# A four-layer graph network on one core: first-layer inputs loaded in the edge-list block, score products as five groups on two sets of PSUM banks

## The chip, the cores and the metric

The kernel runs on one core of one Trainium2 chip. The metric is the device time of one execution in microseconds (us), and its median before the change is 2970.07 us over three runs (2968.24 to 2970.22). Engines are named as the profile names them: PE is TensorE's matmul side and PEld its weight load, DVE is VectorE, ACT is ScalarE, POOL is GpSimd, SP is SyncE. A name with a q behind it (SPq, PEq) is the sequencer of that engine, which waits, branches and issues DMAs.

## The reference

There are 3125 nodes with 64 features and 103125 edges sorted by their receiving node. Four layers follow each other, each ending in `x = layernorm(x + layer(x))`. The change touches only the start of the first:

```python
proj = einsum('nf,hfg->nhg', x, w_proj)                 # 4 heads
delta = proj[sender] - proj[receiver]
radial_logits = einsum('ehf,hf->eh', delta, radial_score) - scale * edge_len
tangential_logits = einsum('ehf,hf->eh', delta, tangential_score)
...  # segment softmax of both over the receiver, summed over delta
```

The part of a logit that depends on the receiver cancels in the softmax. What is left of a sender is the product of its 64 features with one vector per head and score, `u = sum_g w_proj[h, f, g] * score[h, g]`. So the kernel needs `u` (64 x 8) and `x @ u` for all nodes (3125 x 8), once.

## The kernel before

Nodes are laid out as 25 windows of 128 (`NW` is 25, `P` 128). The program is a sequence of blocks; in a block each engine has its own instruction stream, ordered by semaphores, and all engines meet in a barrier at its end. Where a phase frees its semaphores (L65, L66), a second barrier follows.

The order of work is this.

- The edge-list block (L541 to L701) loads source, destination and weight of all edges (SP, L548 to L552), turns them on PE (L692), and then runs some 80 small DVE instructions in a chain up to L684, which pack the loops' bounds. SP waits for two tables (L557), stores them (L558, L559) and waits for everything it has issued (L560, L561).
- The score block (L722 to L743) starts after the two barriers. SP issues six loads: `w_proj`, the two scores, the distance scale and the node features `x` in two pieces (L726 to L732). DVE waits for all six (L738), then multiplies and reduces twice to get `u` (L740, L741) and scales the edge lengths (L742, L743).
- `node_linear` (L124 to L178) computes `x @ u` in five turns of `U` = 5 windows, as a hardware loop on each engine. In a turn POOL copies five windows to `staged` (L140), PE transposes them into PSUM `turned_ps` (L150), ACT copies that to SBUF `turned` (L165), PE multiplies it by `u` into `out_ps` (L155), and DVE copies the result to `logits` (L174). There is one `turned_ps`, one `turned` and one `out_ps`.
- The following block (L747 to L810) takes the largest and smallest logit over all nodes, exponentiates, scales the features by it, and stores the table that the edges gather from (L757).
- The first edge loop (`edges0`, from L860) gathers a table row per edge with indirect DMAs that POOL issues (L880), 888 of them. Then come the end of the first layer, the second layer (`rounds`), and the second edge loop with its own 888 indirect DMAs (L2066). The last stage (from L2394) holds a group of five transposes, a copy and five products like that of `node_linear`, written out and not as a loop (L2445, L2417, L2453), with a bias row and 64 output columns.

All SP DMAs of these blocks go through SP's one queue, in program order.

Of the kernel before, what the change touches and what calls it, by code (L numbers as in the profile page):

```python
# [14 lines left out]
P = 128  # L15
# [193 lines left out]
def build(nc, a, out):  # L209
    with Phase(nc, "all") as whole:  # L210
# [285 lines left out]
        with Phase(nc, "first") as first:  # L496
# [7 lines left out]
            with Borrowed(nc, "setup", flat) as ph:  # L504
                x_in = ph.sb("x_in", [P, NW, F])
                lens = ph.sb("lens", [P, TT])
                with Borrowed(nc, "strips", flat, ph.at) as pt:
                    FULL = TILES // P * P
# [32 lines left out]
                    with nc.Block() as block:  # L541

                        @block.sync
                        def _(sp):
# [13 lines left out]
                            sp.dma_start(src_kept, src_i[:, :]).then_inc(s_kept, 16)  # L558
                            sp.dma_start(dst_kept, dst_f[:, :]).then_inc(s_kept, 16)  # L559
                            sp.wait_ge(s_ld, 144)  # L560
                            sp.wait_ge(s_kept, 48)  # L561

                        @block.gpsimd
# [138 lines left out]

                w_proj = ph.sb("w_proj", [F, H0, F])
                score = ph.sb("score", [F, 2, H0 * F])
                prod = ph.sb("prod", [F, H0, F])
                u = ph.sb("u", [F, A0])
                neg_c = ph.sb("neg_c", [P, 1])
                logits = ph.sb("logits", [P, NW, A0])
# [5 lines left out]
                factor_t = ph.sb("factor_t", [P, NW, H0])  # L714
                s_ld, s_ch, s_less, s_exp, s_rows = (ph.sem(n) for n in ("s_ld", "s_ch", "s_less", "s_exp", "s_rows"))
                s_top, s_all, s_st, s_neg = ph.sem("s_top"), ph.sem("s_all"), ph.sem("s_st"), ph.sem("s_neg")
# [5 lines left out]
                with nc.Block() as block:  # L722

                    @block.sync
                    def _(sp):
                        sp.dma_start(w_proj[:, :, :], a["L0_gnn_w_proj"].rearrange("h f g -> f h g")).then_inc(s_ld, 16)  # L726
                        for n, name in enumerate(("L0_gnn_radial_score", "L0_gnn_tangential_score")):
                            sp.dma_start(score[:, n], a[name].rearrange("h f -> (h f)").partition_broadcast(F)).then_inc(s_ld, 16)
                        sp.dma_start(neg_c[:, :], a["L0_gnn_radial_distance_scale"].partition_broadcast(P)).then_inc(s_ld, 16)
                        with nc.allow_non_contiguous_dma("rows"):  # L730
                            sp.dma_start(x_in[:, 0:FULLW, :], by_node(a["x"][0:FULLW * P])).then_inc(s_ld, 16)
                            sp.dma_start(x_in[0:RESTW, FULLW, :], a["x"][FULLW * P:N]).then_inc(s_ld, 16)  # L732
                        sp.wait_ge(s_ld, 96)

                    @block.vector
                    def _(dve):
                        step = Chain(dve, s_ch)
                        dve.wait_ge(s_ld, 96)  # L738
                        for n in range(2):
                            step(dve.tensor_tensor(prod[:, :, :], w_proj[:, :, :], score[:, n].rearrange("p (h f) -> p h f", f=F), ALU.mult))  # L740
                            step(dve.tensor_reduce(u[:, n * H0:(n + 1) * H0], prod[:, :, :], AX, ALU.add))  # L741
                        step(dve.tensor_scalar(neg_c[:, :], neg_c[:, :], -1.0, None, ALU.mult))  # L742
                        step(dve.tensor_scalar(lens[:, :], lens[:, :], neg_c[:, 0:1], None, ALU.mult))  # L743

                node_linear(nc, lambda nc, tag: Borrowed(nc, tag, flat, ph.at), "l0", x_in, u[:, :], F, A0, None, logits)

# [1810 lines left out]
```

## Time and profile before

| | us |
|---|---|
| median of three runs | 2970.07 |
| lowest, highest | 2968.24, 2970.22 |
| the profiled execution, its own time | 2972.75 |
| its span, first to last instruction | 2970.9 |
| first edge loop, first to last indirect DMA's start | 144.4 to 1296.3 |
| PE, DVE, POOL busy | 75%, 70%, 60% of the span |

The times of instructions below are counted from the start of the span. A share of busy time is an average over stages that have different limits, so the stretch that the change touches is read by itself, in order of time. An idle time in square brackets is how long the engine had nothing to do before an instruction, with what released it.

### The profile page before, as it was taken

The numbers are of one execution on the slowest core, as the hardware profiler recorded it, in microseconds if no ns is written. First come the engines' busy times: TensorE is split into PE (matmuls) and PEld (weight loads), VectorE is DVE, ScalarE is ACT, GpSimd is POOL, SyncE is SP. The second block draws the span as 40 slices with busy tenths as digits, with TensorE's granted clock in tenths as the row PEclk, the third lists the DMA queues.
The fourth block names the chain that finished last, engine by engine and source line by source line (L and its number), as shares of the span: only waits on it lengthen the run. The fifth ranks groups of instructions, "written<-read, shape, count | busy, mean of one in ns | idle before, by whom it ended". The sixth has DMA issues, their size and how long they took to land. (4 is left out here: it accounts for less than half of the span.)

```text
span 2970.9 us, 64636 instructions
## 1 busy us (share of the span) xinstructions
PE 2225.6 (75%) x13922; PEld 1710.1 (58%) x13923; DVE 2083.0 (70%) x7862; ACT 631.7 (21%) x1180; POOL 1783.2 (60%) x1857
## 2 busy tenths in 40 slices
PE   0288888889888898986799557667676676676748
PEld 0255555555555555555799446656566666565637
DVE  6477777777777777747566557777777777777755
ACT  0323322333222333231000111111111111111100
POOL 0077777777777777730001167777777777777722
PEclk9999999999999999985899555555555555555558
DMA  1144554545545455542000133333333333333330
GB/s 42 55 128 133 141 142 128 142 130 145 141 129 143 126 142 141 134 88 57 20 1 2 35 77 83 81 82 82 81 81 82 81 83 81 81 82 80 82 41 12
DMA packets 425511, 268.62 MB, mean 90 GB/s; under 512 B 334070, under 2 KB 375909, under 8 KB 425445
## 3 DMA queue, kind: packets, MB, share of 16 engines
q0 software_dynamic: 71040, 176.52, 23.6%
q1 hardware_dynamic: 284418, 49.42, 8.8%
q10 hardware_dynamic: 69986, 41.88, 4.6%
q8 instruction: 32, 0.52, 0.1%
q14 instruction: 35, 0.28, 0.0%
HBM read 231.16 MB, written 15.97 MB: 83 GB/s over the span
## 5 line engine op out<-in xcount | busy, mean ns | idle before, releaser
L880 POOL DMA_INDIRECT edges_rows<-table,edges_idx x888 | 862.8, 972 | 290.2 <-issue 221.9
L2066 POOL DMA_INDIRECT all_arena<-table_kv,edges_idx x888 | 855.8, 964 | 276.3 <-issue 255.7
L2258 PE MATMUL edges_acc<-edges_values,edges_into 128*128 128x136 f32 x1776 | 511.4, 461 | 259.7 <-DVE edges_values L2146 237.6
L2258 PEld LDWEIGHTS edges_acc<-edges_values,edges_into 128*128 128x128 f32 x1776 | 416.6, 328 | 307.0 <-DVE edges_values L2146 286.4
L1053 PE MATMUL edges_radial_ps<-edges_rows,edges_into_w 128*128 x1776 | 461.3, 396 | 94.1 <-SPq L897 75.3
L962 DVE TENSOR_SCALAR edges_cell<-edges_ramp,edges_strip_key,first_key 128x400 bf16<-128x400 f16 x1184 | 451.2, 381 | 0.0
L1053 PEld LDWEIGHTS edges_radial_ps<-edges_rows,edges_into_w 128*128 128x128 f32 x1776 | 319.8, 190 | 219.0 <-issue 178.0
L2111 DVE TENSOR_SCALAR edges_ahead<-edges_nodes,edges_starts,edges_dst_f 128x128 bf16<-128x128 f32 x894 | 261.7, 360 | 174.3 <-issue 174.3
L961 DVE TENSOR_SCALAR edges_low<-edges_places,first_src_low 128x128 bf16<-128x128 bf16 x1184 | 332.1, 281 | 0.0
L2192 ACT COPY edges_into_t<-edges_t_ps 128x384 bf16<-128x384 bf16 x298 | 142.9, 480 | 874.0 <-PE edges_t_ps L2226 865.1
L967 DVE TENSOR_SCALAR edges_into_w<-edges_nodes,first_dst_f,first_weight 128x128 f32<-128x128 f32 x888 | 276.1, 368 | 0.0
L1048 PE MATMUL edges_cells_ps<-edges_cell,edges_low 128*128 128x400 bf16 x1184 | 251.2, 335 | 32.9 <-DVE edges_cell L962 25.7
L2120 DVE TENSOR_SCALAR edges_into<-edges_nodes,edges_starts,edges_dst_f 128x128 f32<-128x128 f32 x891 | 257.5, 350 | 20.5 <-PE edges_acc L2258 19.2
L2226 PE MATMUL edges_t_ps<-all_ident,edges_ahead 128*128 128x128 bf16 x894 | 155.1, 312 | 112.2 <-DVE edges_ahead L2111 110.0
L1023 PE MATMUL edges_tan_ps<-all_arena 128*128 128x393 bf16 x1300 | 232.0, 335 | 0.1
L1114 ACT ACT_TABLE_LOAD x50 | 64.2, 1283 | 727.3 <-PE edges_radial_ps L1053 727.3
L2235 PE MATMUL edges_q_ps<-attention_q,edges_into_t 128*128 (+1 forms) x2673 | 206.6, 244 | 0.0
L2226 PEld LDWEIGHTS edges_t_ps<-all_ident,edges_ahead 128*128 128x128 bf16 x894 | 108.8, 144 | 153.2 <-DVE edges_ahead L2111 99.0
L1048 PEld LDWEIGHTS edges_cells_ps<-edges_cell,edges_low 128*128 128x128 bf16 x1184 | 101.3, 98 | 162.9 <-DVE edges_cell L962 105.1
L2235 PEld LDWEIGHTS edges_q_ps<-attention_q,edges_into_t 128*128 128x128 bf16 x2673 | 188.5, 134 | 1.1
L1023 PEld LDWEIGHTS edges_tan_ps<-all_arena 128*128 128x128 fp8e4 x1300 | 129.5, 102 | 87.8 <-issue 4.4
L1159 POOL TENSOR_TENSOR rounds_st<-rounds_st,all_minus_half 128x5 f32<-128x5 f32 x20 | 25.9, 1295 | 226.0 <-DVE rounds_st L1150 226.0
(343 smaller groups left out, 2561.4 us busy)
## 6 DMA issues: line engine op xcount, KB each, us to landing
edges_values<-in_edge_attr SPq DMA_DIRECT2D x888, 32.0 KB
all_arena<-all_arena ACTq DMA_DIRECT2D x50, 400.0 KB
edges_rows<-table,edges_idx POOLq DMA_INDIRECT x888
all_arena<-table_kv,edges_idx POOLq DMA_INDIRECT x888
edges_attr<-in_edge_attr ACTq DMA_DIRECT2D x51, 256.0 KB
edges_bias<-bias_kept SPq DMA_DIRECT2D x296, 12.0 KB
bias_kept<-edges_bias_out ACTq DMA_DIRECT2D x52, 64.0 KB
table<-all_arena SPq DMA_DIRECT2D x1, 3250.0 KB, 11.4
```

Source lines behind the costliest of these rows:

```text
L880: pool.indirect_dma_start(rows[:, n, :], None, table0, bass.IndirectOffsetOnAxis(ap=idx[:, n:n + 1], axis=0)).then_inc(s_rows[g], 16)
L961: dve.tensor_scalar(low[:, h, q, :], places[:, :], src_low[:, bass.ds(tile[q], 1)], None, ALU.is_equal)
L962: last = dve.tensor_scalar(cell[:, h, q, :], ramp[:, :], strip_key[:, q:q + 1], key[:, bass.ds(tile[q], 1)], ALU.add, ALU.is_equal)
L967: last = dve.tensor_scalar(into_w[:, h, j, :], nodes[:, :], dst_f[:, bass.ds(t, 1)], weight[:, bass.ds(t, 1)], ALU.is_equal, ALU.mult)
L1023: last = nc.tensor.matmul(tan_ps[:, 0:3 * TAN], last_count[:, c, :], parts0[:, side * NW + c, :, :].rearrange("p k f -> p (k f)"), start=( ...
L1048: nc.tensor.matmul(cells_ps[:, q, 0:KEY], low[:, h, q, :], cell[:, h, q, :], start=False, stop=True, skip_group_check=True)
L1053: last = nc.tensor.matmul(radial_ps[:, 0:ROW0], into_w[:, h, j, :], rows[:, bass.ds(slot + h * G + j, 1), :].squeeze(1), start=False, stop ...
L2066: pool.indirect_dma_start(rows[:, n, :], None, table_kv, bass.IndirectOffsetOnAxis(ap=idx[:, n:n + 1], axis=0)).then_inc(s_rows[g], 16)
L2111: last = dve.tensor_scalar(ahead[:, h, j, :], nodes[:, :], starts[:, bass.ds(w, 1)], dst_f[:, bass.ds(base + h * G + j, 1)], ALU.add, ALU. ...
L2226: last = nc.tensor.transpose(t_ps[:, h, j * P:(j + 1) * P], ahead[:, h, j, :], ident16[:, :])
L2235: last = nc.tensor.matmul(q_ps[:, h, j * F:(j + 1) * F], into_t[:, h, j, :], q3[:, bass.ds(w, 1), n, :].squeeze(1), start=(n == 0), stop=( ...
L2258: last = nc.tensor.matmul(acc[:, 0:2 * F + H2], into[:, h, j, :], values[:, h, j, :], start=False, stop=True, skip_group_check=True)
```

## The change

The six loads move from the score block into the edge-list block, behind the two table stores on SP's queue, with a semaphore of their own (`s_first`, 96) that SP waits for before the block ends. Their tiles `w_proj`, `score` and `neg_c` are laid out ahead of the tiles of that block so that they do not overlap them. The score block has no SP part and no wait left. `node_linear` isn't called here any more; its place is taken by a block with five groups written out. PE transposes straight from `x_in`, so POOL's copy to `staged` is gone. There are two `turned_ps`, two halves of `turned` and two `out_ps`, and PE's order is: transposes of group 0, transposes of group 1, products of 0, transposes of 2, products of 1, and so on to the products of 3 and 4.

```diff
@@ -504,6 +504,10 @@
             with Borrowed(nc, "setup", flat) as ph:
                 x_in = ph.sb("x_in", [P, NW, F])
                 lens = ph.sb("lens", [P, TT])
+                w_proj = ph.sb("w_proj", [F, H0, F])
+                score = ph.sb("score", [F, 2, H0 * F])
+                neg_c = ph.sb("neg_c", [P, 1])
+                s_first = ph.sem("s_first_in")
                 with Borrowed(nc, "strips", flat, ph.at) as pt:
                     FULL = TILES // P * P
                     REST = TILES - FULL - 1
@@ -557,8 +561,16 @@
                             sp.wait_ge(s_tab, 2)
                             sp.dma_start(src_kept, src_i[:, :]).then_inc(s_kept, 16)
                             sp.dma_start(dst_kept, dst_f[:, :]).then_inc(s_kept, 16)
+                            sp.dma_start(w_proj[:, :, :], a["L0_gnn_w_proj"].rearrange("h f g -> f h g")).then_inc(s_first, 16)
+                            for n, name in enumerate(("L0_gnn_radial_score", "L0_gnn_tangential_score")):
+                                sp.dma_start(score[:, n], a[name].rearrange("h f -> (h f)").partition_broadcast(F)).then_inc(s_first, 16)
+                            sp.dma_start(neg_c[:, :], a["L0_gnn_radial_distance_scale"].partition_broadcast(P)).then_inc(s_first, 16)
+                            with nc.allow_non_contiguous_dma("rows"):
+                                sp.dma_start(x_in[:, 0:FULLW, :], by_node(a["x"][0:FULLW * P])).then_inc(s_first, 16)
+                                sp.dma_start(x_in[0:RESTW, FULLW, :], a["x"][FULLW * P:N]).then_inc(s_first, 16)
                             sp.wait_ge(s_ld, 144)
                             sp.wait_ge(s_kept, 48)
+                            sp.wait_ge(s_first, 96)
 
                         @block.gpsimd
                         def _(pool):
@@ -700,11 +712,8 @@
                             act.copy(dst_f[:, :], turn_ps[:, 1, 0:TT]).then_inc(s_copied, 1)
                             act.copy(lens[:, :], turn_ps[:, 2, 0:TT]).then_inc(s_copied, 1)
 
-                w_proj = ph.sb("w_proj", [F, H0, F])
-                score = ph.sb("score", [F, 2, H0 * F])
                 prod = ph.sb("prod", [F, H0, F])
                 u = ph.sb("u", [F, A0])
-                neg_c = ph.sb("neg_c", [P, 1])
                 logits = ph.sb("logits", [P, NW, A0])
                 top = ph.sb("top", [P, 2, A0 + 1])
                 top_all = ph.sb("top_all", [P, 2, A0 + 1])
@@ -712,7 +721,7 @@
                 rows = ph.sb("rows", [P, NW, ROW0])
                 factor_r = ph.sb("factor_r", [P, NW, H0])
                 factor_t = ph.sb("factor_t", [P, NW, H0])
-                s_ld, s_ch, s_less, s_exp, s_rows = (ph.sem(n) for n in ("s_ld", "s_ch", "s_less", "s_exp", "s_rows"))
+                s_ch, s_less, s_exp, s_rows = (ph.sem(n) for n in ("s_ch", "s_less", "s_exp", "s_rows"))
                 s_top, s_all, s_st, s_neg = ph.sem("s_top"), ph.sem("s_all"), ph.sem("s_st"), ph.sem("s_neg")
                 s_part, s_cast = ph.sem("s_scaled"), ph.sem("s_parts")
 
@@ -720,29 +729,55 @@
                     return parts0[:, k * NW:(k + 1) * NW, n, :]
 
                 with nc.Block() as block:
-
-                    @block.sync
-                    def _(sp):
-                        sp.dma_start(w_proj[:, :, :], a["L0_gnn_w_proj"].rearrange("h f g -> f h g")).then_inc(s_ld, 16)
-                        for n, name in enumerate(("L0_gnn_radial_score", "L0_gnn_tangential_score")):
-                            sp.dma_start(score[:, n], a[name].rearrange("h f -> (h f)").partition_broadcast(F)).then_inc(s_ld, 16)
-                        sp.dma_start(neg_c[:, :], a["L0_gnn_radial_distance_scale"].partition_broadcast(P)).then_inc(s_ld, 16)
-                        with nc.allow_non_contiguous_dma("rows"):
-                            sp.dma_start(x_in[:, 0:FULLW, :], by_node(a["x"][0:FULLW * P])).then_inc(s_ld, 16)
-                            sp.dma_start(x_in[0:RESTW, FULLW, :], a["x"][FULLW * P:N]).then_inc(s_ld, 16)
-                        sp.wait_ge(s_ld, 96)
 
                     @block.vector
                     def _(dve):
                         step = Chain(dve, s_ch)
-                        dve.wait_ge(s_ld, 96)
                         for n in range(2):
                             step(dve.tensor_tensor(prod[:, :, :], w_proj[:, :, :], score[:, n].rearrange("p (h f) -> p h f", f=F), ALU.mult))
                             step(dve.tensor_reduce(u[:, n * H0:(n + 1) * H0], prod[:, :, :], AX, ALU.add))
                         step(dve.tensor_scalar(neg_c[:, :], neg_c[:, :], -1.0, None, ALU.mult))
                         step(dve.tensor_scalar(lens[:, :], lens[:, :], neg_c[:, 0:1], None, ALU.mult))
 
-                node_linear(nc, lambda nc, tag: Borrowed(nc, tag, flat, ph.at), "l0", x_in, u[:, :], F, A0, None, logits)
+                with Borrowed(nc, "logit", flat, ph.at) as pt:
+                    turned = pt.sb("turned", [F, 2, U * P])
+                    turned_ps = [pt.ps(f"turned_ps{i}", [F, 8, P]) for i in range(2)]
+                    out_ps = [pt.ps(f"out_ps{i}", [P, U, A0]) for i in range(2)]
+                    s_tps, s_turned, s_lin, s_read = (pt.sem(n) for n in ("s_turned_ps", "s_turned", "s_linear", "s_read"))
+                    GR = NW // U
+                    with nc.Block() as block:
+
+                        @block.tensor
+                        def _(pe):
+                            for g in range(GR + 1):
+                                if g < GR:
+                                    if g >= 2:
+                                        pe.wait_ge(s_turned, g - 1)
+                                    for n in range(U):
+                                        last = nc.tensor.transpose(turned_ps[g % 2][:, n, :], x_in[:, g * U + n, :], ident[:, :])
+                                    last.then_inc(s_tps, 1)
+                                if g:
+                                    pe.wait_ge(s_turned, g)
+                                    if g >= 3:
+                                        pe.wait_ge(s_read, g - 2)
+                                    for n in range(U):
+                                        last = nc.tensor.matmul(out_ps[(g - 1) % 2][:, n, :], turned[:, (g - 1) % 2, n * P:(n + 1) * P], u[:, :],
+                                                                start=True, stop=True)
+                                    last.then_inc(s_lin, 1)
+
+                        @block.scalar
+                        def _(act):
+                            for g in range(GR):
+                                act.wait_ge(s_tps, g + 1)
+                                if g >= 2:
+                                    act.wait_ge(s_lin, g - 1)
+                                act.copy(turned[:, g % 2, :].rearrange("p (n i) -> p n i", i=P), turned_ps[g % 2][:, 0:U, :]).then_inc(s_turned, 1)
+
+                        @block.vector
+                        def _(dve):
+                            for g in range(GR):
+                                dve.wait_ge(s_lin, g + 1)
+                                dve.tensor_copy(logits[:, g * U:(g + 1) * U, :], out_ps[g % 2][:, :, :]).then_inc(s_read, 1)
 
                 with nc.Block() as block:
```

## Rows read from the trace of the kernel before

**Rows 1.** The page: the span, and the granted clock of 40 slices.

```profile
span 2970.9 us, 64636 instructions
...
PEclk9999999999999999985899555555555555555558
```

**Rows 2.** The page's costliest groups: POOL's indirect DMAs of both edge loops.

```profile
L880 POOL DMA_INDIRECT edges_rows<-table,edges_idx x888 | 862.8, 972 | 290.2 <-issue 221.9
L2066 POOL DMA_INDIRECT all_arena<-table_kv,edges_idx x888 | 855.8, 964 | 276.3 <-issue 255.7
```

**Rows 3.** Timeline, 35 to 73 us: start, duration, engine, line, operation, idle time before.

```profile
35.21 0.58 DVE L615 TENSOR_SCALAR all_arena<-all_arena 128x812 int32<-128x812 int32 x1
35.56 0.43 SPq L559 DMA_DIRECT2D dst_kept<-first_dst_f  x1
...
60.01 0.17 DVE L684 COPY all_visits<-all_arena 1x25 int32<-1x25 int32 x1
61.17 0.79 SPq L726 DMA_DIRECT2D all_arena<-in_L_gnn_w_proj  x1
...
64.38 2.24 SPq L732 DMA_DIRECT2D all_arena<-in_x  x1
69.63 0.42 DVE L740 TENSOR_TENSOR all_arena<-all_arena 64x256 f32<-64x256 f32 x1 [9.45 <-DMA all_arena<-in_x]
...
71.61 0.64 DVE L743 TENSOR_SCALAR all_arena<-all_arena 128x812 f32<-128x812 f32 x1
```

**Rows 4.** Timeline, 73 to 97 us: first two turns of `node_linear`, and its end.

```profile
73.07 0.45 POOL L140 COPY all_arena<-all_arena 128x320 f32 x1 [38.44 <-PEq L144]
...
73.66 1.25 PE L150 MATMUL l_turned_ps<-all_ident,all_arena 128*64 128x128 f32 x5 [54.59 <-POOL all_arena L140]
75.02 0.69 ACT L165 COPY all_arena<-l_turned_ps 64x640 f32<-64x640 f32 x1 [53.60 <-PE l_turned_ps L150]
...
75.76 2.30 PE L155 MATMUL l_out_ps<-all_arena 64*128 64x8 f32 x10 [0.85 <-ACT all_arena L165]
...
77.99 1.27 PE L150 MATMUL l_turned_ps<-all_ident,all_arena 128*64 128x128 f32 x5
...
93.17 2.30 PE L155 MATMUL l_out_ps<-all_arena 64*128 64x8 f32 x10 [0.85 <-ACT all_arena L165]
95.64 0.20 DVE L174 TENSOR_SCALAR all_arena<-l_out_ps 128x40 f32 x1 [4.15 <-PE l_out_ps L155]
96.60 0.51 DVE L770 TENSOR_REDUCE all_arena<-all_arena 128x8 f32<-128x200 f32 x1 [0.75 <-PEq L66]
```

**Rows 5.** SP's waits, 30 to 75 us: for what, us in total, times, longest.

```profile
SPq L561 <- DMA dst_kept<-first_dst_f: 3.1, 1, 3.1
SPq L722 <- DMA all_arena<-in_x: 3.0, 1, 3.0
```

**Rows 6.** Lines L155 and L150 alone: single durations in ns, least, median, most.

```profile
L155 PE MATMUL l_out_ps<-all_arena x50: 357/358/379, 75.8 to 95.1; 64*128 64x8 f32 x50
...
L150 PE MATMUL l_turned_ps<-all_ident,all_arena x25: 394/420/421, 73.7 to 91.9; 128*64 128x128 f32 x25
```

**Rows 7.** Timeline, 2875 to 2880 us: the written-out group of the last stage.

```profile
2875.17 1.27 PE L2445 MATMUL last_banks_turned_ps<-all_ident,attention_attn 128*64 128x128 f32 x5 [17.01 <-DVE attention_attn L2472]
2877.22 2.40 PE L2453 MATMUL last_banks_out_ps<-attention_w_sq,last_turned 65*128 65x64 f32 x10 [0.78 <-ACT last_turned L2417]
```

**Rows 8.** Windows: us, busy PE, PEld, DVE, ACT, POOL, granted clock, DMA share, GB/s.

```profile
70.00:80.00 10.00, 4.75 (x20) 3.63 (x20) 2.28 (x7) 1.31 (x2) 1.35 (x3) 1.00 0.00 0
...
1600.00:1620.00 20.00, 20.00 (x236) 19.98 (x234) 11.05 (x29) 2.10 (x4) 1.35 (x2) 1.00 0.01 2
1620.00:1635.00 15.00, 11.01 (x120) 10.60 (x117) 8.26 (x20) 1.74 (x3) 2.67 (x2) 0.99 0.00 1
1635.00:1650.00 15.00, 10.09 (x40) 8.23 (x41) 10.82 (x24) 2.06 (x3) 3.41 (x3) 0.50 0.00 1
```

**Rows 9.** Line L880 alone: durations in ns, least, median and most.

```profile
L880 POOL DMA_INDIRECT edges_rows<-table,edges_idx x888: 940/947/1297, 144.4 to 1296.3; - x178
```

## The prediction

> **What bounds the kernel now.** I first asked whether time saved at the start can reach the end. Most of the span is two edge loops, each paced by POOL: 888 indirect DMAs of 972 ns on average with 290.2 us of idle time between them, so 1.30 us a piece and 1153 us in the first loop; the second has 855.8 + 276.3 = 1132 us [rows 2]. Their start is what matters, not when in the run it falls. Between the changed stretch and the first loop there are only chains closed by barriers of all engines, and none of them waits for a DMA started before that stretch. So a microsecond taken out before 96.6 us should come off the end too, unless something later answers to it.
>
> Then I read the stretch itself in order of time. The reader is to see two holes. DVE ends the edge-list chain at 60.18, SP issues its first load at 61.17 and its last until 66.62, and DVE gets its first instruction at 69.63, after 9.45 us of idle time that the load of `x` ended [rows 3]. In the product, PE is the busiest engine, but stops before each group of products for 0.85 us, while ACT copies the turned windows [rows 4]. It first starts at 73.66, after POOL's copy. The stretch ends with DVE's L770 at 96.60 [rows 4].
>
> **Part 1, the six loads.** Their wait goes, and what then comes last is the barrier. SP was past it at 61.17; DVE leaves the same barrier. The same pair of barriers at the end of `node_linear` let DVE go 0.76 us after its last instruction (95.84 to 96.60) [rows 4], which would give 60.94. I take 61.17: 69.63 - 61.17 = 8.46 us saved; bounds 8.46 and 8.69.
>
> What the loads cost in their new place: SP's queue is free from 35.99, when the second table store is issued [rows 3]. The six issues took 66.62 - 61.17 = 5.45 us and the last load ended 3.0 us behind the last issue [rows 3, 5]. So they are issued by 41.4 and landed by about 44.5. The stores share the DMA engines for a while, and SP waited 3.1 us for them [rows 5]; even with that added, the loads are in by 48, 12 us before DVE reaches 60.18. Nothing stands behind them on SP's queue but the waits at the block's end, and the stores are ahead of them. If that cover were gone, each microsecond past 60.18 would be paid in full. For DVE working beside the transfers, the nearest row is L615, 0.58 us for 812 elements while a store is issued [rows 3]; I take nothing, with 0.3 us against me as the other end (some 25 us of DVE work slowed by 1%).
>
> DVE's six instructions from L740 to L743 stay as they are: 69.63 to 72.25, 2.62 us [rows 3].
>
> **Part 2, the start of the product.** Before, DVE ended at 72.25; then came the barrier, POOL's loop start, its copy at 73.07 of 0.45 us, and PE at 73.66 [rows 3, 4]. POOL's idle time there was ended by PE's sequencer (L144, the increment that PE gives ahead of its loop), so PE was through the barrier before 73.07. Afterwards PE's first transpose waits for nothing but the barrier. A barrier pair took 0.76 us [rows 4], so this single one ends no earlier than about 72.6. I take 72.85: 0.8 us saved, bounds 0.56 and 1.0.
>
> **Part 3, the five groups.** Before, PE ran from 73.66 to 95.47, 21.81 us: a first turn of 2.10 to the products, then 2.23 from products to transposes, and 2.12 back, of which 0.85 idle [rows 4]. A single transpose shows 0.42 us and five together 1.25 to 1.27, so their pitch is 0.21; a single product instruction 0.36 and ten together 2.30, pitch 0.216 [rows 4, 6]. Five transposes thus take 1.07 from start to next start, ten product instructions 2.16, and with a change of kind 2.23. For transposes followed at once by products no row exists. It lies between 1.07 (nothing extra) and 1.27 (the last one drained first); I take 1.17, the pitch plus a little more than the 0.07 that the other change of kind costs.
>
> The new order gives 1.07 (group 0) + 4 x 1.17 (groups 1 to 4, each ahead of products) + 3 x 2.23 (products 0 to 2, each ahead of transposes) + 2.16 + 2.30 (products 3 and 4) = 16.90 us. Saved: 21.81 - 16.90 = 4.9 us, bounds 4.4 and 5.3.
>
> That sum needs ACT's copies hidden. A group of products may start 0.85 us after its transposes end (0.69 us copy and two handoffs) [rows 4]. Products 0 stand behind group 1's transposes, which end a good microsecond after group 0's, so about 0.2 us is to spare. Later copies have at least a group of products to hide in. If the spare is negative it costs a few tenths once. DVE's copy is 0.20 us against 3.4 us until its PSUM buffer is written again. The end is unchanged: the last products, then DVE 0.17 us later, then the barriers [rows 4]. POOL's five copies of 0.45 us go and free nothing, because four of them ran behind PE's products.
>
> That written-out code runs no slower than the loop is shown by the last stage, where five transposes take 1.27 us, and the wait before the products is 0.78 [rows 7].
>
> **Sum.** 8.46 + 0.8 + 4.9 = 14.2 us; with all bounds on one side 13.1 and 15.0. The profiled execution took 2972.75 us, so its like would take 2958.6; it was 2.7 us above the median of 2970.07. Against the median: 2970.07 - 14.2 = **2955.9 us**. A difference of 0.2%, 5.9 us, is about what a measurement of this kernel can tell from no change.
>
> **Rivals.**
>
> *The clock of a later stage is dealt anew.* After the first loop the granted clock moves between 1.2 and 2.4 GHz, and the slices show mixed levels there [rows 1]. PE is fully busy at 1.00 up to 1620 us, 73% busy in the next 15 us, and then at 0.50 [rows 8]. If that fall came 10 us earlier or later in the program, ten microseconds of PE work at half rate, 5 us, would be lost or won: 2961 or 2951. For it: the fall lies close behind a stretch of dense work. Against it: four executions lie within 4.5 us. I give 0.08 to the loss and 0.05 to the gain. The Trainium skill (TensorE: Matmul & The Clock Gate, Part 1: The HAM clock gate) says that the window by which the gate is set is free-running and doesn't restart with the kernel, so an earlier start can't keep the old phase; the rows show the level changing but not its phase, and by that rule the small shifts would differ from one execution to the next.
>
> *Only the loads' part is won.* If each group of products still waited for its copy (a semaphore that comes late, or a PSUM write held by a reader), the product block would keep its turns: 2970.07 - 8.46 = 2961.6. Against it: the waits named in the diff are all due well before they are reached. Chance 0.04.
>
> *The gain is swallowed.* The change does what it says, but the first loop starts no earlier, or settles 14 us later. The first loop's indirect DMAs would need 14.2 / 888 = 16 ns more each; their mean is already 25 ns above their median of 947 [rows 2, 9], so such amounts exist. Result 2970, chance 0.05.
>
> *Slower.* The same mechanism, larger. The long indirect DMAs, up to 1297 ns [rows 9], come when DVE and POOL meet in a bad phase. The instruction streams ahead of the loops change in length and the tiles shift; if the share of long ones doubled, the first loop would gain 888 x 25 ns = 22 us: 2955.9 + 22 = 2978. It decides from 8 ns on both loops' 1776 DMAs (14.2 us), and it is slower by over 0.2% from 11 ns. Against it: the loops' code and data are untouched and start from the same barrier. Chance 0.04.
>
> **How the numbers follow.** The forecast has 0.74. Faster by over 0.2%: the forecast, both clock cases and the loads alone, 0.91. Within 0.2%: 0.05. Slower: 0.04. The forecast's own bounds are 2955.1 to 2957.0, to which the spread of medians adds a microsecond. The range takes in the clock cases and the loads alone: 2951 to 2962, leaving out 0.09 and what small shifts I haven't named.
>
> **What would show it.** In the trace after: SP's six loads right behind L559's store and landed before 50 us; DVE's first product within 1.1 us of the chain's last instruction; PE without idle time between groups and some 17 us from first transpose to last product; no POOL copy; DVE's first reduction near 82.4 us instead of 96.60. Then the first indirect DMA at 144.38 - 14.2 = 130.2 and both loops as long as before. Wrong would be: DVE waiting for a load at 60 us, PE waiting for ACT in every group, or a first loop whose POOL mean is not 972 ns.

## The result, and the profile after

The changed kernel takes 2961.69 us (median of 20 runs, 2954.46 to 2967.55), the kernel before 2970.08 us (median of 20 beside them, one disturbed run of 7149 us left out of the comparison). The ratio is 0.997, with a 95% interval of 0.9963 to 0.9977. The change is 8.4 us faster by the two medians, and 6.8 to 11.0 us by the interval, where 14.2 us was forecast. The profiled execution took 2963.00 us by its own time, 9.75 us less than that of before.

The page of after, to be held against [rows 1, 2]; the columns of the two groups are busy us, mean ns, idle us before:

```profile
span 2960.8 us, 64538 instructions
...
L915 POOL DMA_INDIRECT edges_rows<-table,edges_idx x888 | 867.7, 977 | 291.2 <-issue 227.9
L2101 POOL DMA_INDIRECT all_arena<-table_kv,edges_idx x888 | 855.9, 964 | 276.6 <-issue 257.3
```

The second loop's line stands where it stood. The first loop's has grown by 4.9 us of busy time and 1.0 us of idle time, on lines that the change didn't touch. That is the missing part. First the changed stretch itself, in the timeline of after (start, duration, engine, line, operation, idle time before), to be read against [rows 3, 4]:

```profile
35.38 0.79 SPq L564 DMA_DIRECT2D all_arena<-in_L_gnn_w_proj  x1
...
38.71 2.25 SPq L570 DMA_DIRECT2D all_arena<-in_x  x1
...
59.36 0.17 DVE L696 COPY all_visits<-all_arena 1x25 int32<-1x25 int32 x1
60.56 0.42 DVE L737 TENSOR_TENSOR all_arena<-all_arena 64x256 f32<-64x256 f32 x1 [1.04 <-PEq L66]
...
63.72 2.31 PE L757 MATMUL logit_turned_ps<-all_ident,all_arena 128*64 128x128 f32 x10 [45.58 <-PEq L731]
...
65.96 2.30 PE L764 MATMUL logit_out_ps<-all_arena 64*128 64x8 f32 x10
...
68.19 1.27 PE L757 MATMUL logit_turned_ps<-all_ident,all_arena 128*64 128x128 f32 x5
...
69.40 2.30 PE L764 MATMUL logit_out_ps<-all_arena 64*128 64x8 f32 x10
...
76.26 4.43 PE L764 MATMUL logit_out_ps<-all_arena 64*128 64x8 f32 x20
...
80.73 0.20 DVE L780 COPY all_arena<-logit_out_ps 128x40 f32<-128x40 f32 x1 [1.94 <-PE logit_out_ps L764]
81.66 0.51 DVE L805 TENSOR_REDUCE all_arena<-all_arena 128x8 f32<-128x200 f32 x1 [0.73 <-PEq L66]
...
129.41 1.30 POOL L915 DMA_INDIRECT edges_rows<-table,edges_idx  x1 [0.20 <-issue]
```

DVE's wait of 9.45 us for `x` is now 1.04 us for the barrier. PE's lines follow each other with no idle time and no wait for ACT. The first indirect DMA starts at 129.41 instead of 144.38, 14.97 us earlier, of which 0.65 us was there before the change could act (the list chain ends at 59.36 and not at 60.01, and was as far ahead before the first of the moved loads was issued). By stage, from the two timelines (starts in us):

| stage | before | after | saved | forecast |
|---|---|---|---|---|
| last list instruction to DVE's first product | 9.62 | 1.20 | 8.42 | 8.46 |
| first product to PE's start | 4.03 | 3.16 | 0.87 | 0.8 |
| PE's start to its end | 21.81 | 16.97 | 4.84 | 4.9 |
| PE's end to the first reduction | 1.13 | 0.97 | 0.16 | 0 |
| first reduction to first indirect DMA | 47.78 | 47.75 | 0.03 | 0 |
| first loop, first to last indirect DMA | 1151.92 | 1157.75 | -5.83 | 0 |
| from there to the second loop's first | 424.11 | 421.95 | 2.16 | 0 |
| second loop | 1125.26 | 1125.31 | -0.05 | 0 |
| from its last to the end of the span | 125.18 | 126.34 | -1.16 | 0 |

The front gave 14.3 us, as forecast. The first loop took 5.8 us back.

Inside that loop, DVE's groups of 120 to 1310 us differ in two lines. L975 (L940 before) is DVE's first engine instruction in each of the 25 windows of 128 nodes, and each time DVE's sequencer has set up the window's registers ahead of it. L993 (L958 before) copies the indices for the next chunk. After:

```profile
L975 DVE TENSOR_SCALAR edges_nodes<-edges_nodes 128x128 f32<-128x128 f32 x25 | 6.4, 257 | 98.8 <-issue 98.8
...
L993 DVE COPY edges_idx<-first_src_i x296 | 60.6, 205 | 99.4 <-issue 64.3 <-PE edges_radial_ps L1088 20.6 <-SPq L932 14.4
```

and before:

```profile
L940 DVE TENSOR_SCALAR edges_nodes<-edges_nodes 128x128 f32<-128x128 f32 x25 | 5.7, 228 | 102.2 <-issue 102.2
...
L958 DVE COPY edges_idx<-first_src_i x296 | 60.6, 205 | 92.3 <-issue 76.5 <-PE edges_radial_ps L1053 14.0 <-SPq L897 1.6
```

Ahead of that instruction DVE is idle for 102.2 us in 25 windows before and for 98.8 us after, and "issue" says that it waits for nothing the profile shows, which here is its own sequencer. Taken singly, the first window's idle time is 10.71 us before and 10.27 after, the 24 others are 3.79 to 3.82 and 3.67 to 3.70. So DVE's first instruction comes 0.12 us sooner at each change of window in the changed kernel, and yet DVE then waits longer for rows and for PE (99.4 against 92.3 us), and POOL's DMAs are longer. I used this sum of 25 idle times as the mark of a loop in all that follows: in all 14 traces it is either 98.8 to 98.9 or 102.0 to 102.4 us.

### The profile page after: what moved, and what is told of

It reads as the page before. It is cut to its first block and busy times, and to the rows that moved or that the text cites. A ratio compares the mean times of both kernels' runs of the same rounds, so it can differ in the third digit from the quotient of the medians.

```text
span 2960.8 us, 64538 instructions
## 1 busy us (share of the span) xinstructions
PE 2223.9 (75%) x13922; PEld 1710.8 (58%) x13923; DVE 2085.0 (70%) x7862; ACT 631.9 (21%) x1180; POOL 1785.7 (60%) x1852
## 5 line engine op out<-in xcount | busy, mean ns | idle before, releaser
L915 POOL DMA_INDIRECT edges_rows<-table,edges_idx x888 | 867.7, 977 | 291.2 <-issue 227.9
L2227 ACT COPY edges_into_t<-edges_t_ps 128x384 bf16<-128x384 bf16 x298 | 142.5, 478 | 875.9 <-PE edges_t_ps L2261 862.8
L1002 DVE TENSOR_SCALAR edges_into_w<-edges_nodes,first_dst_f,first_weight 128x128 f32<-128x128 f32 x888 | 271.9, 371 | 0.0
```

Source lines behind the costliest of these rows:

```text
L915: pool.indirect_dma_start(rows[:, n, :], None, table0, bass.IndirectOffsetOnAxis(ap=idx[:, n:n + 1], axis=0)).then_inc(s_rows[g], 16)
L1002: last = dve.tensor_scalar(into_w[:, h, j, :], nodes[:, :], dst_f[:, bass.ds(t, 1)], weight[:, bass.ds(t, 1)], ALU.is_equal, ALU.mult)
```

## The experiments

The question was what makes the first loop longer, since nothing in it was changed. The theories, with the letters that the recorded expectations use: **place** (S: the instruction streams ahead of the loop have another length, so the loop's code lies elsewhere), **start time** (T: the loop meets something else at 129 us than at 144 us), **chip** (C: executions on some chips have it), **one part** (the groups or the loads bring it), and later **total length** of DVE's stream (L) and **moment** of entry (M: some tenths of a us).

### The two parts alone

e1 keeps the early loads and calls `node_linear` again:

```diff
-                with Borrowed(nc, "logit", flat, ph.at) as pt:
...
+                node_linear(nc, lambda nc, tag: Borrowed(nc, tag, flat, ph.at), "l0", x_in, u[:, :], F, A0, None, logits)
```

> Only the loads are moved; the product stays the loop of five turns. The stretch up to the first reduction over the logits should lose 9.1 us (DVE waits 1.0 us and not 9.5). If removed time arrives at the end whole: 2970.1 - 9.1 = 2961 us. If the first edge loop's length depends on how the instruction streams lie (theory S), it may differ from 1151.9 us although nothing in it is changed; SP's, DVE's and PE's streams change little here, so S expects a loop close to that of the kernel before. If it depends on when the loop starts (theory T), a loop that starts 9 us earlier should be as long and as scattered as that of the changed kernel, 1157.8 us, and the total some 2966 us.

e2 is the kernel before with the written-out groups in place of that call:

```diff
-                node_linear(nc, lambda nc, tag: Borrowed(nc, tag, flat, ph.at), "l0", x_in, u[:, :], F, A0, None, logits)
+                with Borrowed(nc, "logit", flat, ph.at) as pt:
...
```

> Only the product is changed into five overlapped groups, the loads stay where they were. PE from first transpose to last product 17.0 us and not 21.8, and its start 0.8 us sooner: 5.7 us less up to the first reduction over the logits. Whole gain at the end: 2964.4 us. Theory S (streams): POOL's, ACT's, DVE's and PE's streams lie as in the changed kernel, so the first edge loop should have its length, 1157.8 us, and its scatter of 13 us over executions: 2970 us. Theory T (start time): a start 5.7 us earlier gives something between, 2964 to 2968 us.

e1: 2962.74 us, ratio 0.9974 (0.9964 to 0.9984). Its first indirect DMA starts at 135.57, 8.8 us earlier than before, and its median is 7.8 us below that of the kernel before beside it (2970.56), so most of it reaches the end; its loop takes 1153.15 us. e2: 2970.47 us, ratio 0.9998 (0.9989 to 1.0007). Its first indirect DMA starts at 138.47, 5.9 us earlier, and all of that is lost (0.1 us between the medians): its loop takes 1159.29 us. Their rows for the group at the window's start:

```profile
L937 DVE TENSOR_SCALAR edges_nodes<-edges_nodes 128x128 f32<-128x128 f32 x25 | 5.7, 230 | 102.4 <-issue 102.4
```

```profile
L978 DVE TENSOR_SCALAR edges_nodes<-edges_nodes 128x128 f32<-128x128 f32 x25 | 6.6, 263 | 98.9 <-issue 98.9
```

The first is e1's and has the value of before, the second is e2's and has that of after. The long loop comes with the written-out groups, also without the loads. But the groups are over long before the loop begins, so it's something that they leave behind.

### The same kernel again, and held back

e3 is the changed kernel once more. e4 lets it start its loop as late as before, with three fills of a tile that isn't in use yet:

```diff
                         step = Chain(dve, s_ch)
+                        step(dve.memset(rows[:, :, :], 0.0))
+                        step(dve.memset(rows[:, :, :], 0.0))
+                        step(dve.memset(rows[:, 0:HOLD, :], 0.0))
```

> The changed kernel once more, for a second trace. Median near 2961.7 us, spread of about 10 us. If the loss sits in the first edge loop in every execution, that loop is again over 1154 us, and at other places than in the first trace (there one turn of 17.77 us at 833 us, and 45 turns that were 0.06 us longer each). If the first trace was a chance hit, the loop is 1152 us and the loss sits elsewhere.

> The changed kernel with three fills of a tile that is not used yet put ahead of the score products on DVE, about 15 us of dead time, so that the first edge loop starts when it did in the kernel before (144 us). DVE's stream is three instructions longer, all others are those of the changed kernel. Theory T: the loop is that of the kernel before, 1151.9 us, scatter 4 us, total 2970 us. Theory S: the loop is that of the changed kernel, 1157.8 us, total 2961.7 + 15 = 2976.7 us, scatter 10 us.

e3: 2962.57 us, ratio 0.9977 (0.9968 to 0.9986), loop 1160.24 us, mark 98.8. The changed kernel has the long loop again. e4: 2974.37 us, ratio 1.001 (1.0001 to 1.0019). Its first indirect DMA starts at 147.03, which is 17.6 us later than in after, but it ends only 11.8 us behind e3's median: its loop takes 1152.31 us, as before. These rows are e4's, DVE at the window's start and POOL's DMAs:

```profile
L979 DVE TENSOR_SCALAR edges_nodes<-edges_nodes 128x128 f32<-128x128 f32 x25 | 5.7, 228 | 102.1 <-issue 102.1
```

```profile
L919 POOL DMA_INDIRECT edges_rows<-table,edges_idx x888 | 861.7, 970 | 291.7 <-issue 223.1 <-DVE edges_idx L997 68.6
```

So the written-out groups don't bring the long loop by themselves. e4 can't tell the later start from the three instructions that it adds to DVE's stream. e1 already speaks against the start time (short at 135.6, while e2 is long at 138.5); the next runs add instructions at no cost in time.

### Cheap instructions ahead of the loop

e5, e6 and e7 add one, two and four fills of a single column, each about 0.06 us, ahead of the score products:

```diff
                         step = Chain(dve, s_ch)
+                        for i in range(PAD):
+                            dve.memset(top[:, 0, i:i + 1], 0.0)
```

> The changed kernel with one fill of a single column put on DVE ahead of the score products (60 ns). The last runs split the kernels by DVE's restart at a half-window of the first edge loop (from the end of the overflow maximum to the next copy of indices): 4.95 and 5.71 us in turn with a loop of 1152 to 1153 us in before, loads only and held, 4.97 to 5.06 and 5.63 to 5.69 us with 1158 to 1160 us in the changed kernel and groups only. DVE's static stream has 174 instructions ahead of that loop in the long ones, 175, 175 and 177 in the short ones. Theory S, now narrowed to DVE's stream: one instruction more gives the 4.95 / 5.71 pattern, a loop of 1152 to 1153 us and 2961.7 - 5 = 2956.7 us. Theory T (start time): the loop starts where that of the changed kernel does and stays at 1158 us, total 2961.7 us.

> The changed kernel with two such fills, DVE stream 176. Theory S: short loop too, if only every fourth place is bad; 2956.8 us. If odd and even places differ: long loop, 2962 us. Theory T: 1158 us, 2962 us.

> The changed kernel with four such fills, DVE stream 178, that is 174 + 4. Theory S with a period of four instructions: the long loop again, 1158 us, 2962 us. Theory S with any longer period: short loop, 1152 us, 2957 us. Theory T: 1158 us, 2962 us.

e8 is the kernel before with one DVE instruction less at that place, which was meant to give it the count of after and e2:

```diff
-                        step(dve.tensor_scalar(neg_c[:, :], neg_c[:, :], -1.0, None, ALU.mult))
-                        step(dve.tensor_scalar(lens[:, :], lens[:, :], neg_c[:, 0:1], None, ALU.mult))
+                        step(dve.tensor_scalar(lens[:, :], lens[:, :], neg_c[:, 0:1], -1.0, ALU.mult, ALU.mult))
```

> The kernel before with the two instructions that negate the scale and multiply the edge lengths by it made one, so that DVE's stream ahead of the first edge loop has 174 instructions as in the changed kernel; nothing else differs and the loop starts 0.2 us earlier. Theory S: DVE's restarts 4.97 to 5.06 and 5.63 to 5.69 us, loop 1158 us instead of 1152, total 2970.1 - 0.2 + 5.5 = 2975.4 us, and a wider scatter. Theory T: the kernel before, 1152 us, 2969.9 us.

| | median, us | ratio (95%) | first indirect DMA | first loop, us | mark |
|---|---|---|---|---|---|
| e5, one more | 2955.51 | 0.9952 (0.9938 to 0.9965) | 129.74 | 1153.04 | 102.3 |
| e6, two more | 2955.36 | 0.9954 (0.9939 to 0.997) | 129.72 | 1151.85 | 102.1 |
| e7, four more | 2955.16 | 0.9952 (0.9937 to 0.9967) | 129.99 | 1153.98 | 102.0 |
| e8, before less one | 2969.51 | 1.0002 (0.9993 to 1.0011) | 144.27 | 1151.44 | 102.2 |

One instruction of 0.06 us makes the loop short, at a start of 129.7 us: the start time is out, and the forecast's 14.2 us is reached (0.9952 of 2970.1 is 2955.8). One, two and four instructions give medians within half a microsecond, so neither odd and even places differ nor does the long loop come back after four.

e8 missed its expectation: a long loop was expected and a short one came. The 174 of the expectation doesn't count all that DVE's stream holds. The trace also records what DVE's sequencer does itself (registers, branches, waits), which the timeline leaves out. Counted once each, the recorded instructions ahead of the loop's L975 are 190 in after and e2, 192 in before and e1, and 191 in e8. So e8 didn't reach the place of after; it would have had to lose two.

### On one chip, and three other causes

The pads had run on another chip than e3. So the changed kernel (e9) and the one with one pad (e10) ran on one chip, with two more. e11 puts the extra instruction behind both loops, in the last stage, so that DVE's stream is as long in all as e10's, and the first loop's code lies as in after:

```diff
+                        dve.memset(y[:, 0, 0:1], 0.0)
                         shares(0)
```

e12 adds no instruction, but lengthens a fill at the start of DVE's list chain, so that everything behind it moves by about 0.1 us:

```diff
-                            dve.memset(x_in[:, NW - 1, :], 0.0).then_inc(s_zero, 1)
+                            dve.memset(x_in[:, NW - 3:NW, :], 0.0).then_inc(s_zero, 1)
```

> The changed kernel unchanged, so that it stands on one chip beside the one-fill version. Theory S (where DVE's instructions lie): restarts of 4.97 to 5.06 and 5.63 to 5.69 us, loop 1157 to 1160 us, 2962 us. Theory C (the chip: the short loops of the last set were all seen on another one than the long ones): the pattern 4.95 and 5.71, a loop of 1152 to 1154 us and 2956 us.

> The one-fill version again, same chip as the changed kernel. Theory S: 4.95 and 5.71, 1152 to 1154 us, 2955.5 us. Theory C: no different from the changed kernel beside it.

> The changed kernel with the one fill put at the start of DVE's part of the last stage, behind both edge loops, so that DVE's stream is one instruction longer in all but the first loop lies where it does in the changed kernel. Theory S: the loop stays long, 1157 to 1160 us, 2962 us. Theory L (what counts is how the whole program is laid out in memory, the lengths of the streams): short loop, 1152 to 1154 us, 2956 us.

> The changed kernel with one fill of the edge-list block three times as large (0.1 us more of time, no instruction more). Theory S: long loop, 2962 us. Theory M (what counts is the moment in which the loop is entered, which the fill moved by a tenth of a microsecond): short loop, 1152 to 1154 us, 2956 us.

| | median, us | ratio (95%) | first loop, us | mark |
|---|---|---|---|---|
| e9, after | 2963.63 | 0.997 (0.9958 to 0.9983) | 1157.79 | 98.9 |
| e10, one pad ahead | 2959.05 | 0.9952 (0.9939 to 0.9965) | 1152.49 | 102.3 |
| e11, pad in the last stage | 2963.80 | 0.9974 (0.9961 to 0.9987) | 1156.10 | 98.9 |
| e12, longer fill | 2966.72 | 0.9981 (0.9972 to 0.9989) | 1158.23 | 98.8 |

The chip is out (e9 and e10 ran on the same one), the total length of the stream is out (e11), and so is the moment of entry (e12). The moment can be read still more closely: e5 and e12 both start their loop at 129.74, and one is short and the other long. The intervals of e9 and e10 overlap a little; what carries the comparison is that the loops in the traces differ by 5.3 us, and that four versions with pads have a ratio of 0.9952 to 0.9954 and three runs of the changed kernel one of 0.997 to 0.9977. What is left is the place: one DVE instruction ahead of the loop. Here is e10's first loop, the window's start, the index copies, and POOL's DMAs:

```profile
L978 DVE TENSOR_SCALAR edges_nodes<-edges_nodes 128x128 f32<-128x128 f32 x25 | 5.7, 228 | 102.3 <-issue 102.3
...
L996 DVE COPY edges_idx<-first_src_i x296 | 59.0, 199 | 92.3 <-issue 75.5 <-PE edges_radial_ps L1091 13.6 <-SPq L935 3.2
```

```profile
L918 POOL DMA_INDIRECT edges_rows<-table,edges_idx x888 | 860.2, 969 | 293.4 <-issue 225.2 <-DVE edges_idx L996 67.9 <-PE edges_radial_ps L1091 0.3
```

All three are at the values of before or close to them: 102.3 (before 102.2) and 92.3 (92.3) us idle, 969 ns a DMA (972).

### Where in the loop it acts

The timelines show one window change. After, from 836 us:

```profile
836.76 0.15 DVE L957 TENSOR_TENSOR all_over_most<-all_over_most,edges_over_now 128x1 f32<-128x1 f32 x1
...
840.61 0.26 DVE L975 TENSOR_SCALAR edges_nodes<-edges_nodes 128x128 f32<-128x128 f32 x1 [3.69 <-issue]
...
842.56 0.17 DVE L993 COPY edges_idx<-first_src_i  x1 [1.61 <-issue]
...
843.55 0.98 POOL L915 DMA_INDIRECT edges_rows<-table,edges_idx  x1 [2.73 <-DVE edges_idx L993]
```

and the same one in e10, from 832 us:

```profile
832.34 0.15 DVE L960 TENSOR_TENSOR all_over_most<-all_over_most,edges_over_now 128x1 f32<-128x1 f32 x1
...
836.30 0.23 DVE L978 TENSOR_SCALAR edges_nodes<-edges_nodes 128x128 f32<-128x128 f32 x1 [3.81 <-issue]
...
838.22 0.18 DVE L996 COPY edges_idx<-first_src_i  x1 [1.62 <-issue]
```

DVE's first instruction waits 3.69 us in the one and 3.81 us in the other. In the first of them POOL then waits 2.73 us for DVE's indices, in e10 it is 0.81 us. Such stalls are no more than a share of POOL's idle time, which is 291.2 us in after and 290.2 before.

The sequencer's own records tell where the 0.12 us lie. The register work itself is as long in both kinds (3.51 to 3.52 us at the median, where the gap isn't in it). But in every trace, at all 25 windows, one gap of about 0.12 us stands somewhere in the steps around L975, and it moves by one instruction for each instruction that DVE's stream has more or less ahead of the loop:

| kernels | instructions ahead of L975 | where the gap stands | first loop, us |
|---|---|---|---|
| e7 | 194 | ahead of the first register step of L972 | 1154.0 |
| e4 | 193 | ahead of the second register step of L972 | 1152.3 |
| before, e1, e6 | 192 | ahead of the semaphore step, L973 | 1151.9 to 1153.2 |
| e5, e8, e10 | 191 | ahead of L975 | 1151.4 to 1153.0 |
| after, e2, e3, e9, e11, e12 | 190 | behind L975 | 1156.1 to 1160.2 |

(Lines as in after.) Ahead of an instruction the gap delays it in full. Behind L975 it passes while L975 runs, in part: the copy of the indices for which POOL waits comes 5.64 to 5.65 us after the old window's last instruction, against 5.72 us in all the others. So what POOL sees is 0.07 us, and not 0.12, and at the other change, to a window's second side, it sees no gain (4.98 to 4.99 us against 4.94 to 4.98).

Most of the 5.8 us between before and after isn't a stall of POOL, but the length of the DMAs (in e2 and e3, as in e11, POOL's idle time has grown too, by 3 to 4 us):

| | DVE's idle time at a change, us | mean indirect DMA, ns | over 1000 ns | first loop, us |
|---|---|---|---|---|
| before, e1, e4, e5 to e8, e10 | 3.81 | 969 to 973 | 145 to 170 | 1151.4 to 1154.0 |
| after, e2, e3, e9, e12 | 3.69 | 975 to 977 | 174 to 183 | 1157.8 to 1160.2 |
| e11 | 3.69 | 973 | 162 | 1156.1 |

The first and the last column keep the two kinds apart in every trace. The two in the middle do so but for e11, the shortest of the long loops, whose DMAs are within the range of the short ones while its POOL waits longer between them than before (293.3 against 290.2 us). The median is the same (946 to 949 ns); the mean is carried by those that take 1 to 1.3 us. The line of after, durations least, median and most, against [rows 9]:

```profile
L915 POOL DMA_INDIRECT edges_rows<-table,edges_idx x888: 940/946/1297, 129.4 to 1287.2; - x178
```

Could the other place make the sequencer fetch code anew at each window? The Trainium skill (Runtime: NRT & Kernel Launch, Instruction fetch mechanics) says that a taken branch to code outside the two pages at hand has to wait for a transfer of the target page. The instruction queues of after, 160 to 1280 us (packets, MB, share of 16 engines), show two packets:

```profile
q8 instruction: 1, 0.02, 0.0%
q14 instruction: 1, 0.01, 0.0%
```

e10 has the same two lines in that stretch, e2 (long) and before (short) three packets each. So there is no fetch at each of some two dozen window changes, in either kind, and that rule isn't the cause.

The traces also tell which DMAs are the long ones. In after, the 183 over 1000 ns ran beside DVE's `edges_into_w` instructions (L1002) for 827 ns on average, the 705 others for 159 ns. DMAs that don't touch these instructions take 954 to 957 ns on average in all 14 traces, those that do take 993 to 1001 ns in the short loops and 1001 to 1010 ns in the long ones. Of the 888 DMAs 326 to 340 touch them in the eight short loops, and 349 to 373 in the six long ones. So in a long loop POOL's DMAs and these DVE instructions lie differently to each other.

**What stays open.** That the place of DVE's code ahead of the loop decides is shown by adding one instruction there and elsewhere, and by the gap that moves with it. What the gap is, no run shows. Why only the place behind L975 costs 5 us is open too: that an earlier restart of 0.07 us shifts POOL's DMAs against DVE's `edges_into_w` fits the counts above, but it is a correlation over 14 traces (8 short, 6 long). No run moved the DVE restart by itself.

## Why the prediction was right and wrong

**What bounds the kernel** was read rightly in one half. Everything ahead of the loops does count: the first loop began 14.97 us earlier. The half that failed is the sentence that a microsecond taken out before 96.6 us should come off the end too. It rested on the absence of a wait across the barrier. The loop answered to something that no wait shows.

**Part 1, the loads: right.** 8.42 us against 8.46. They were issued from 35.38 to 40.96 (forecast by 41.4). SP's wait puts their landing at about 44.3 (forecast 44.5), against 3.1 us that it waits for the stores before [rows 5]:

```profile
SPq L573 <- DMA all_arena<-in_x: 3.3, 1, 3.3
```

The cover was 15 us. The 0.3 us held against it for DVE working beside the transfers didn't come. The list chain ended 0.65 us earlier, but it was 0.66 us ahead before the loads were issued: from L615 (L627 in after; 35.21 and 34.55 us) to the start of its last instruction it took 24.80 us in both kernels.

**Part 2, the start of the product: right.** 0.87 us against 0.8, inside 0.56 to 1.0.

**Part 3, the groups: right, term by term.** 16.97 us from PE's start to its end, against 16.90. The order that had no row before, five transposes followed at once by products, took 1.21 us (68.19 to 69.40), where I took 1.17 between 1.07 and 1.27. ACT's copies were hidden, the first one too: PE shows no idle time ahead of L764.

**The sum** of the three, 14.2 us, stands against 14.3 us measured at the loop's door, 0.16 of it behind PE's end. The time failed by 5.8 us because a fourth term was taken at nothing: the first loop. By the trace it is 4.9 us of busy POOL and 1.0 us of idle POOL. 2955.9 + 5.8 = 2961.7 us is the measured median; that it fits to the tenth is luck, since 5.8 us comes from one execution of each kernel, and the loops of e3 and e9 are 8.3 and 5.9 us longer than that of before. The 2.16 us won in the middle and the 1.16 lost at the end of the profiled execution are of the size by which single executions differ: the middle stretch took 418.6 us in e1, 421.0 in e2 and 424.7 in e3.

**The rivals.** "Only the loads' part is won" gives 2961.6 and so names the right time for the wrong reason: the groups did save their 4.9 us in their own stretch, and PE doesn't wait for ACT. The gain was partly swallowed by the mechanism of the third and fourth rivals. They named it (the streams ahead of the loops change in length, and POOL's DMAs get longer) and asked for 16 or 25 ns each; the trace gave 5 ns on one of the two loops. I argued against them with "the loops' code and data are untouched and start from the same barrier". That is the step that failed. It is true and doesn't carry: code untouched in text may still lie elsewhere, and e5 shows that one more instruction ahead of it, 0.06 us long, is worth about 5 us (0.9970 against 0.9952 on one chip in e9 and e10, and 1157.8 against 1152.5 us of loop). Both rivals together had 0.09, and the case in between, a few ns a DMA and a gain partly lost, wasn't priced.

**The range**, 2951 to 2962, holds 2961.69, but that is luck. Its upper end was set for the clock's loss and for the loads alone, and neither happened; the forecast's own bounds, 2955.1 to 2957.0, miss the time by 4.7 us.

**The clock rival** isn't needed. Its price, 5 us, is that of 10 us of time at half rate; ten microseconds of PE work would have cost ten. The middle stretch, where it would act, went down by 2.16 us in after, and varies by 6 us over the kernels; the rows don't tie that to the clock. [Rows 8] shows a clock of 1.00 at 70 to 80 us that wasn't granted (see the end); the sum isn't touched, as the same pitches held before and after.

**What would show it** worked: the list of rows to look at had "a first loop whose POOL mean is not 972 ns", and that was the one that came.

Faster than both kernels is e5's version, the change with one cheap DVE instruction ahead of the score products: 0.9952 (0.9938 to 0.9965) and again 0.9952 (0.9939 to 0.9965) of the time before in two comparisons, and the versions with two and four such instructions agree. Against the changed kernel's 0.9963 to 0.9977 the intervals of e5 and e10 overlap by 0.0002; it is the four runs together, all within 0.9952 to 0.9954, that set them apart.

## What to carry to other kernels

Time saved ahead of a long loop isn't banked until the loop's own length has been compared; read the mean of its pacing instruction and the idle time at its register work before and after, even where nothing in it changed. If it moved, put one cheap instruction ahead of the loop and measure again, before any theory. In a loop of some hundred short steps that two engines share, leave a few tenths of a percent for this in the range.

## What the runs showed of the hardware that was not expected

The length of an untouched loop depends on where its code lies: 1151.4 to 1154.0 us in eight traces and 1156.1 to 1160.2 in six, told apart by DVE's 3.81 or 3.69 us at a window change, with nothing between, and one DVE instruction of 0.06 us moves it from one kind to the other. A gap of 0.12 us in DVE's stream moves by one instruction with each instruction added ahead of the loop.

The second is the clock in the product stretch. Windows of 60 to 85 us, columns as in [rows 8], after and then e10:

```profile
60.00:85.00 25.00, 16.98 (x75) 14.67 (x75) 6.64 (x16) 3.43 (x5) 0.00 (x0) 0.50 0.00 1
```

```profile
60.00:85.00 25.00, 16.98 (x75) 14.68 (x75) 6.28 (x16) 3.42 (x5) 0.00 (x0) 1.00 0.00 1
```

The granted clock is recorded as 0.50 in the one (1.2 GHz) and as 1.00 in the other (2.4 GHz), and PE is busy for 16.98 us in both, with the same instructions. The Trainium skill (TensorE: Matmul & The Clock Gate, Part 1: The HAM clock gate) says that the phase of the gate differs from one execution to the next, and that matmuls take longer at the lower level. The second is so here, for fp32 transposes too. These are the four at the start of the first loop in after, the other 192 of the same line and shape, and those at the start in e10 (durations in ns, least, median, most):

```profile
L1035 PE MATMUL edges_attr_ps<-all_ident,edges_attr x4: 417/418/444, 130.7 to 131.4; 128*128 128x128 f32 x4
L1035 PE MATMUL edges_attr_ps<-all_ident,edges_attr x192: 272/273/303, 161.9 to 1267.6; 128*128 128x128 f32 x192
L1038 PE MATMUL edges_attr_ps<-all_ident,edges_attr x3: 421/421/447, 131.4 to 131.9; 128*128 128x128 f32 x3
```

In after the first four stand at a recorded 0.50 and the 192 at 1.00. Those of e10 take 421 ns at a recorded 1.00, so they ran at the lower level and the record is wrong there. The record of the clock holds nothing before 142.6 us in e10, 142.5 in e12 and 156.6 in the kernel before, where L1000's four transposes at 145.7 us take 421 ns too; where it holds nothing, a window shows 1.00. In the other eleven traces it begins at 17 to 19 us and has 0.50 through the changed stretch. With equal durations in all of them, the stretch ran at the lower level in every kernel, and the 1.00 of an early window is to be held against the duration of a known instruction.
